# First layer's window-attention maxima: mask added and maximum taken per head by one VectorE instruction

## The chip, the cores and the metric

The kernel runs on one core of one Trainium2 chip. The metric is the device time of one execution in microseconds. A core has a matrix engine (TensorE, PE in the rows, with its weight loads as PEld), VectorE (DVE), ScalarE (ACT), GpSimd (POOL) and SyncE (SP), which starts most DMAs. TensorE writes only to PSUM, eight banks of 512 fp32 numbers per partition.

## What is computed

Two transformer layers over eight sequences ("batches") of 512 tokens by 256. The change lies in the first one, in its sliding-window attention (16 heads of 16, window 64):

```
scores = einsum('bqhd,bkhd->bhqk', q, k) / sqrt(D)
allowed = (t[None,:] <= t[:,None]) & (t[None,:] >= t[:,None] - WINDOW)
attn = softmax(where(allowed, scores, -inf)); win = attn @ v
lin  = linear_attention_causal(taylor(q @ Wqf), taylor(k @ Wkf), v)
x    = x + ga * (concat([lin, win]) @ Wout)        # then a gated feed-forward part
```

The second layer has causal softmax attention with rotary positions and a large feed-forward part (256 to 1024, 1024 to 1024 twice, and back).

## The kernel before, in words

**Quads.** Heads are handled four at a time; a batch has four such quads, so the first layer has 32. In `qT` and `kT` the four heads of a quad lie on four groups of 32 partitions, so that four products with 32 rows each share TensorE. One spare row of each head carries minus the row's maximum, so that the scores come out of TensorE with the maximum taken off and ScalarE needs only an `Exp`.

**Steps of a quad n.** `tq`, `tk` turn queries and keys; `fold` makes `mT` for the linear part; `wm.n.0` and `wm.n.1` make scores for the maxima, in two pieces (query tiles 0 to 2: widths 128, 192, 192 for each head; query tile 3: width 192); `again` turns the queries once more, now with the maxima in the spare row, and so waits for both `wm`; `lin.n.0/1/2` and `win.n.0/1` are the scores proper; `lv`, `wv` the products with the values; `lh`, `wh` the turn back. Per batch there are also `hT`, `qk`, `v` (norm and projections), `turn`, `out` (output projection), `xT`, `r`, `kk`, `last` (feed-forward), and `wt` steps that turn the second layer's weights.

**The wide room.** PSUM banks 0 to 3 form one room, "wide". `wm.n.0`, `wm.n.1`, `lin.n.0/1/2` and `win.n.0/1` all use it, seven fills per quad, one after another: a fill may begin only when the reader of the last one is done. ScalarE reads `lin` and `win` (lines 817 to 828), VectorE reads `wm` (lines 667 to 671). Banks 4 and 5 collect value products, banks 6 and 7 (`m0`, `m1`) take all other steps in turn.

**Mask and maximum before.** In `window_maxima` TensorE first multiplies the identity with the mask tile `bandr` (0 or -1e30), four products of 512 columns in `wm.n.0` and four of 192 in `wm.n.1` (line 976), and adds the score products to that (line 979). VectorE then takes the maxima with three wide reductions per quad (lines 667, 669, 671), writing minus the maximum.

**What sets the order.** Each engine runs its instructions in program order. One list of steps (the "plan") gives the order for all of them. It is unrolled from the tables `BODY0` and `BODY1`, one pass per batch, where `+1` or `+2` behind a step says that it runs that many passes later; the lists `START` and `TURN` replace the unrolled order at the beginning and where the layers meet. Until the second layer's feed-forward part can start, only its attention steps (`1:max`, `1:att`, in the same wide room) are there to run.

Of the kernel before, what the change touches and what calls it, by code (L numbers as in the profile page):

```python
# [140 lines left out]
tq.0 tk.0 win.3.1+1 turn.0+1 fold.0 wm.0.0 lv.3.1+1 lv.3.2+1 turn.2+1 wt.0+2 wm.0.1 wv.3.0+1 wv.3.1+1 lin.0.0 lh.3+1 v.0 again.0 lin.0.1 wh.3+1 v.1  # L141
win.0.0 turn.1+1 tq.1 lv.0.0 tk.1 lin.0.2 turn.3+1 fold.1 wm.1.0 out.0+1 wm.1.1 stats-1 out.1+1 mod again.1 lin.1.0 wv.0.0 lv.0.1 win.0.1 wt.1+2
lv.0.2 win.1.0 tq.2 lh.0 lv.1.0 lin.1.1 tk.2 fold.2 wv.0.1 wm.2.0 wt.2+2 rows.0-35 lv.1.1 wt.3+2 xT.0+1 rows.1+1 wm.2.1 flag+8 xg wh.0 xT.1+1 lin.1.2
wv.1.0 win.1.1 again.2 tq.3 lin.2.0 lv.1.2 r.0+1 lin.2.1 tk.3 fold.3 wv.1.1 lin.2.2 norm-1 lh.1 lv.2.0 wm.3.0 r.1+1 kk.0+1 wt.4+2 win.2.0 wh.1 kk.1+1
hT.0-1 wm.3.1 hT.1-1 wt.5+2 lv.2.1 rms-1 win.2.1 again.3 qk.0-1 qk.1-1 wt.6+2 lin.3.0 wv.2.0 wv.2.1 lv.2.2 lin.3.1 wh.2 qk.2-1 last.0+1 win.3.0 lh.2
last.1+1 qk.3-1 lin.3.2 lv.3.0
# [3 lines left out]
def first_layer(nc, ctx, room_ctx, kept, plan, fills, x_in_dram, norm_w, Wq, Wk, Wv, Wqf, Wkf, Wout, W_r, W_k, W_v, mu_r, mu_k, c, wmod, x_mid, next_weights, rope):  # L150
# [344 lines left out]
    def vector(dve):  # L495
# [66 lines left out]
        def run(step):  # L562
# [16 lines left out]
            elif name == "masks":  # L579
                dve.wait_ge(s_masks, 1)  # L580
                nc.vector.tensor_copy(kept.causalr[:], plain_causal)
                nc.vector.tensor_copy(bandr[:], plain_band).then_inc(s_round, 1)
# [577 lines left out]
h1.0.3.1+3 values.1.1+2 values.1.2+2 max.3.1+2 h2.0.0.0+3 h2.0.0.1+3 h2.0.1.0+3 att.2.0+2 h2.0.1.1+3 h2.0.2.0+3 max.3.2+2 h2.0.2.1+3 h2.0.3.0+3  # L1160
h2.0.3.1+3 att.2.1+2 heads.1+2 split.1+3 last.0.0+3 again.3+2 values.2.0+2 att.2.2+2 stats+1 values.2.1+2 att.3.0+2 last.0.1+3 values.2.2+2 att.3.1+2
heads.2+2 up.1.0+3 up.1.1+3 values.3.0+2 att.3.2+2 values.3.1+2 norm+1 up.1.2+3 up.1.3+3 values.3.2+2 hT+1 up.1.4+3 heads.3+2 up.1.5+3 proj.0+1
proj.1+1 up.1.6+3 tq.0+1 tk.0+1 proj.2+1 tq.1+1 tk.1+1 up.1.7+3 proj.3+1 tq.2+1 tk.2+1 h1.1.0.0+3 tq.3+1 tk.3+1 h1.1.0.1+3 h1.1.1.0+3 turn.0+2
max.0.0+1 h1.1.1.1+3 h1.1.2.0+3 max.0.1+1 h1.1.2.1+3 turn.1+2 h1.1.3.0+3 max.0.2+1 h1.1.3.1+3 out.0+2 again.0+1 max.1.0+1 h2.1.0.0+3 h2.1.0.1+3
out.1+2 att.0.0+1 h2.1.1.0+3 h2.1.1.1+3 max.1.1+1 h2.1.2.0+3 h2.1.2.1+3 h2.1.3.0+3 h2.1.3.1+3 xT+2 split.0+2 last.1.0+3 att.0.1+1 last.1.1+3
values.0.0+1 max.1.2+1 up.0.0+2 ga+1 up.0.1+2 att.0.2+1 up.0.2+2 again.1+1 max.2.0+1 up.0.3+2 up.0.4+2 values.0.1+1 values.0.2+1 att.1.0+1 up.0.5+2
up.0.6+2 att.1.1+1 heads.0+1 up.0.7+2 values.1.0+1 att.1.2+1 h1.0.0.0+2 max.2.1+1 h1.0.0.1+2 h1.0.1.0+2 h1.0.1.1+2 max.2.2+1 h1.0.2.0+2 h1.0.2.1+2
# [4 lines left out]
0:stats.0 0:norm.0 0:mod0.0 0:hT.0.0 0:masks.0 0:hT.0.1 0:rows.0.0 0:rms.0 0:qk.0.0 0:qk.0.1 0:qk.0.2 0:qk.0.3 0:wturn.0.0 0:tq.0 0:tk.0 0:fold.0  # L1172
0:wm.0.0 0:v.0.0 0:wm.0.1 0:wturn.0.1 0:wturn.0.2 0:lin.0.0 0:again.0 0:v.0.1 0:lin.0.1 0:lv.0.0 0:tq.1 0:tk.1 0:win.0.0 0:fold.1 0:xg.0 0:lv.0.1
0:wm.1.0 0:wt.0.0 0:wt.0.1 0:wv.0.0 0:wm.1.1 0:win.0.1 0:lin.0.2 0:again.1 0:tq.2 0:stats.1 0:lin.1.0 0:tk.2 0:wv.0.1 0:fold.2 0:lin.1.1 0:lv.0.2
0:lin.1.2 0:norm.1 0:wm.2.0 0:wh.0 0:lh.0 0:lv.1.0 0:wm.2.1 0:mod.0 0:win.1.0 0:hT.1.0 0:lv.1.1 0:lv.1.2 0:lin.2.0 0:win.1.1 0:again.2 0:wt.1.0
0:lin.2.1 0:wv.1.0 0:wv.1.1 0:lh.1 0:win.2.0 0:wh.1 0:tq.3 0:lv.2.0 0:win.2.1 0:tk.3 0:turn.0.0 0:lin.2.2 0:hT.1.1 0:fold.3 0:wm.3.0 0:wv.2.0 0:lv.2.1
0:wv.2.1 0:wm.3.1 0:lv.2.2 0:wh.2 0:rms.1 0:again.3 0:lin.3.0 0:qk.1.0 0:qk.1.1 0:win.3.0 0:qk.1.2 0:qk.1.3 0:lin.3.1 0:tq.4 0:lh.2 0:wv.3.0 0:lin.3.2
0:tk.4 0:fold.4 0:wm.4.0 0:v.1.0 0:lv.3.0 0:wm.4.1 0:lv.3.1 0:win.3.1 0:again.4 0:tq.5 0:lin.4.0 0:wv.3.1 0:lv.3.2 0:tk.5 0:lin.4.1 0:v.1.1 0:turn.0.2
0:lin.4.2 0:fold.5 0:lh.3 0:wm.5.0 0:wh.3 0:lv.4.0 0:lv.4.1 0:wm.5.1 0:turn.0.1 0:wt.1.1 0:lin.5.0 0:turn.0.3 0:again.5 0:tq.6 0:win.4.0 0:tk.6
0:lv.4.2 0:stats.2 0:fold.6 0:wm.6.0 0:out.0.0 0:wm.6.1 0:out.0.1 0:lin.5.1 0:lh.4 0:lv.5.0 0:xg.1 0:again.6 0:win.4.1 0:wv.4.0 0:win.5.0 0:lv.5.1  # L1180
0:tq.7 0:tk.7 0:lin.5.2 0:fold.7 0:win.5.1 0:xT.0.0 0:wv.4.1 0:norm.2 0:wm.7.0 0:wh.4 0:hT.2.0 0:wv.5.0 0:wv.5.1 0:wm.7.1 0:hT.2.1 0:rms.2 0:wh.5
0:win.6.0 0:again.7 0:qk.2.0 0:lv.5.2 0:win.6.1 0:qk.2.1 0:xT.0.1 0:lin.6.0 0:qk.2.2 0:qk.2.3 0:lin.6.1 0:lh.5 0:lv.6.0 0:wv.6.0 0:lin.6.2 0:wv.6.1
0:lv.6.1 0:lin.7.0 0:tq.8 0:v.2.0 0:win.7.0 0:tk.8 0:r.0.0 0:lv.6.2 0:lin.7.1 0:fold.8 0:v.2.1 0:win.7.1 0:r.0.1 0:wm.8.0 0:wh.6 0:lh.6 0:lv.7.0
0:wv.7.0 0:wm.8.1 0:kk.0.0 0:lin.7.2 0:kk.0.1 0:lin.8.0 0:lv.7.1 0:again.8 0:tq.9 0:lin.8.1 0:tk.9 0:fold.9 0:lv.7.2 0:wv.7.1 0:lin.8.2 0:last.0.0
0:win.8.0 0:lh.7 0:last.0.1 0:wh.7 0:wm.9.0 0:turn.1.0 0:lv.8.0 0:turn.1.2 0:turn.1.1 0:wm.9.1 0:lv.8.1 0:turn.1.3 0:again.9 0:win.8.1 0:lv.8.2
0:stats.3 0:tq.10 0:tk.10 0:lin.9.0 0:out.1.0 0:fold.10 0:wm.10.0 0:lh.8 0:out.1.1 0:lin.9.1 0:lv.9.0 0:wv.8.0 0:win.9.0 0:wv.8.1 0:lv.9.1 0:rows.0.1
0:xT.1.0 0:wm.10.1 0:wh.8 0:xT.1.1 0:lin.9.2 0:wv.9.0 0:win.9.1 0:again.10 0:tq.11 0:xg.2
# [4 lines left out]
0:win.26.1 0:norm.7 0:lv.26.1 0:wv.26.0 0:wm.27.0 0:hT.7.0 0:kk.5.0 0:hT.7.1 0:wm.27.1 0:kk.5.1 0:rms.7 0:lin.27.0 0:again.27 0:qk.7.0 0:wv.26.1
0:lv.26.2 0:win.27.0 0:qk.7.1 0:qk.7.2 0:wt.17.0 0:lin.27.1 0:lh.26 0:qk.7.3 0:win.27.1 0:lv.27.0 0:tq.28 0:tk.28 0:lin.27.2 0:fold.28 0:wh.26
0:wm.28.0 0:wv.27.0 0:v.7.0 0:lin.28.0 0:wt.17.1 0:v.7.1 0:wm.28.1 0:lv.27.1 0:wv.27.1 0:again.28 0:lin.28.1 0:tq.29 0:last.5.0 0:lin.28.2 0:lv.27.2
0:tk.29 0:wt.18.0 0:win.28.0 0:lh.27 0:fold.29 0:lv.28.0 0:wm.29.0 0:last.5.1 0:lv.28.1 0:wm.29.1 0:turn.6.0 0:turn.6.2 0:win.28.1 0:wt.18.1
# [856 lines left out]
```

## Time and profile before

| what | us |
|---|---|
| median of 3 runs | 2113.1 (2112.88 to 2118.12) |
| profiled execution, its own time | 2113.57 |
| span of its trace | 2111.8 |
| TensorE busy | 1993.2 (94%) |
| VectorE busy | 1241.8 (59%) |
| ScalarE busy | 943.9 (45%) |
| GpSimd busy | 519.5 (25%) |
| first layer | about 0 to 820 |
| layers meet, attention of the second alone | about 820 to 1000 |

The busy share of an engine is an average over stages with different limits. The timeline views give start, duration, engine, line and shape of instructions merged by form, and in brackets how long the engine had been idle and what ended that. From the start of one group to the start of the next on an engine that never idles is what a group costs it; the duration itself is some hundredths longer, since instructions overlap at their ends. One fp32 product is two records on TensorE, one fp32r product one record.

### The profile page before, as it was taken

The page shows a single profiled execution, that of the slowest core. Times are in us where ns is not written, and L with a number is a line of the kernel's source. Part 1 is how long each engine was busy: PE and PEld are TensorE (multiplying, and loading weights), DVE is VectorE, ACT ScalarE, POOL GpSimd, SP SyncE. Part 2 cuts the span into 40 slices and gives each one's busy share as a digit, 9 for nine tenths or more (in the row PEclk, how much of TensorE's full clock was granted, in tenths as well). Part 3 has the DMA queues.
Part 4 walks back from the last instruction along what each step waited for, and adds up shares of the span by engine and source line. Part 5 has one row for each costly group of instructions (what it writes and reads, how often), then busy time and mean ns, then how long its engine had stood idle before and what let it go on. Part 6 is the DMA issues. An engine that isn't in the chain of part 4 may idle for free.

```text
span 2111.8 us, 41909 instructions
## 1 busy us (share of the span) xinstructions
PE 1993.2 (94%) x17257; PEld 1456.0 (69%) x17257; DVE 1241.8 (59%) x2211; ACT 943.9 (45%) x1306; POOL 519.5 (25%) x676
## 2 busy tenths in 40 slices
...
GB/s 183 27 5 24 24 20 54 71 43 59 68 80 47 39 63 145 11 6 110 1 7 23 2 5 23 6 6 19 6 6 19 6 23 2 6 14 6 1 13 7
DMA packets 58030, 67.69 MB, mean 32 GB/s; under 512 B 11928, under 2 KB 48752, under 8 KB 57200
## 3 DMA queue, kind: packets, MB, share of 16 engines
...
q8 instruction: 141, 2.31, 0.5%
q14 instruction: 49, 0.40, 0.1%
...
## 4 chain that ended last, share of the span: by engine, by line
PE 82%; DVE 8%; ACT 6%; issue 2%; POOL 0%; SPq 0%; DMA 0%; ACTq 0%; DVEq 0%; POOLq 0%
PE ps L1886 28%; PE ps L1833 4%; PE ps L1821 4%; PE ps L1790 4%; PE ps L990 4%; PE ps L1022 3%; PE ps L1923 3%; PE ps L1849 3%; PE ps L1052 3%; PE ps L937 3%; ACT a_probs L817 3%; PE ps L1074 2%; PE ps L979 2%; PE ps L976 2%; PE ps L1000 2%
## 5 line engine op out<-in xcount | busy, mean ns | idle before, releaser
L1744 ACT ACTIVATE b_acts_exact<-ps,c_s 128x256 f32<-128x256 f32 x256 | 107.5, 471 | 373.6 <-PE ps L1886 373.4
L1886 PE MATMUL ps<-b_acts,b_h1T 128*128 128x256 f32 x2048 | 265.6, 287 | 2.7 <-POOL b_acts L1515 1.9
L1886 PEld LDWEIGHTS ps<-b_acts,b_h1T 128*128 128x128 f32 x2048 | 250.2, 191 | 23.0 <-issue 16.6
L1886 PEld LDWEIGHTS ps<-b_acts,b_h2T 128*128 128x128 f32 x2048 | 248.5, 192 | 20.9 <-issue 17.5
L1886 PE MATMUL ps<-b_acts,b_h2T 128*128 128x256 f32 x2048 | 257.8, 285 | 1.4 <-DVE b_acts L1658 1.4
L439 POOL TENSOR_SCALAR_AFFINE_SELECT a_probs<-a_probs 128x512 f32<-128x512 f32 (+1 forms) x224 | 161.3, 736 | 386.4 <-ACT a_probs L817 225.6
L1507 POOL TENSOR_SCALAR_AFFINE_SELECT b_work<-b_work 128x512 f32<-128x512 f32 x128 | 80.7, 642 | 515.5 <-ACT b_work L1708 515.5
L1708 ACT ACTIVATE b_work<-ps 128x2048 f32<-128x2048 f32 (+1 forms) x96 | 153.2, 1596 | 95.9 <-PE ps L1833 95.1
L817 ACT ACTIVATE a_probs<-ps 128x2048 f32<-128x2048 f32 (+1 forms) x96 | 153.1, 1595 | 84.1 <-PE ps L990 72.9
L1579 DVE TENSOR_REDUCE c_nat<-ps 128x4 f32<-128x2048 f32 (+3 forms) x128 | 188.0, 1490 | 3.3
L1657 DVE CAST b_acts<-b_acts_exact 128x512 fp32r<-128x512 f32 x128 | 55.2, 431 | 218.1 <-ACT b_acts_exact L1744 217.8
L1515 POOL TENSOR_TENSOR b_acts<-c_nat,b_acts 128x256 fp32r<-128x256 f32 x128 | 94.8, 741 | 261.3 <-DVE b_acts L1650 261.3
L1022 PE MATMUL ps<-a_probs,c_va 128*17 128x192 f32 (+4 forms) x2048 | 131.8, 379 | 1.0 <-POOL a_probs L439 0.8
L1821 PE MATMUL ps<-c_kT,c_qT 32*128 32x512 f32 (+3 forms) x1024 | 102.1, 492 | 26.8 <-DVE c_nat L1579 18.7
L1576 DVE TENSOR_TENSOR ps<-ps,c_causalr 128x512 f32<-128x512 f32 x128 | 86.0, 695 | 68.7 <-PE ps L1821 68.4
L1833 PE MATMUL ps<-c_qT,c_kT 32*128 32x512 f32 (+3 forms) x1024 | 98.1, 475 | 19.9 <-DVE c_nat L1579 10.1
L990 PE MATMUL ps<-a_mT,c_kT 32*128 32x512 f32 (+3 forms) x1024 | 99.6, 482 | 10.2 <-DVE c_nat L671 3.8
L1886 PE MATMUL ps<-b_acts,b_w1T 128*128 128x256 f32 x512 | 92.6, 303 | 13.1 <-DVEq L1649 9.3
L1737 ACT ACTIVATE c_nat<-ps,c_s 128x256 f32<-128x256 f32 x128 | 59.6, 475 | 101.3 <-PE ps L1886 71.0
L1886 PEld LDWEIGHTS ps<-b_acts,b_w1T 128*128 128x128 f32 x512 | 69.5, 189 | 36.9 <-DVEq L1649 22.2
L1022 PEld LDWEIGHTS ps<-a_probs,c_va 128*17 128x17 f32 x2048 | 47.6, 97 | 64.1 <-issue 52.4
L1658 DVE TENSOR_TENSOR b_acts<-b_acts_exact,b_acts 128x512 fp32r<-128x512 f32 x128 | 88.7, 693 | 4.4
...
## 6 DMA issues: line engine op xcount, KB each, us to landing
...
```

Source lines behind the costliest of these rows:

```text
L439: return nc.gpsimd.affine_select(out=z, in_=z, compare_op=ALU.is_ge, fill=0.0, base=0, pattern=[[0, blocks_n], [1, cols]], channel_multipl ...
L817: nc.scalar.activation(pb, here[:, :, 0:w], ACT.Square, bias=1.0, scale=0.5).then_inc(att_ready, 1)
L990: ins = nc.tensor.matmul(here[:, i, o:o + S - kb * P], kT[rows_of(i), n % RING, kb * P:(kb + 1) * P], mT[rows_of(i), n % RING, kb * P:S], ...
L1022: ins = nc.tensor.matmul(here[R * i:R * i + HD + 1, kb * P:kb * P + q], va[:, b % 2, kb, 4 * g + i, :], pb[:, first + i * pitch:first + i ...
L1515: nc.gpsimd.tensor_tensor(act_a[:, i, 1], th[i % 2], act_a[:, i, 0].bitcast(F32), ALU.subtract).then_inc(a_ready, 1)
L1579: ins = nc.vector.tensor_reduce(nat[:, t, 0, 4 * g:4 * g + 4, HD:HD + 1], room["wide"][:, :, o:o + (t + 1) * P], AX.X, ALU.max, negate=True)
L1658: nc.vector.tensor_tensor(dst[:, :, 1], z, dst[:, :, 0].bitcast(F32), ALU.subtract).then_inc(h_split, 1)
L1708: ins = nc.scalar.activation(probs[nth % 2][:, 0:4 * w].rearrange("p (h q) -> p h q", q=w), here[:, :, 0:w], ACT.Exp, scale=float(HD) ** -0.5)
L1744: ins = nc.scalar.activation(dst[:, j], here[:, j * HALF:(j + 1) * HALF], ACT.Gelu, scale=s12[:, 2 + (name == "h2"), 2 * i + j:2 * i + j + 1])
L1821: ins = nc.tensor.matmul(here[:, i, o:o + (t + 1) * P], qT[rows_of(i), g, t * P:(t + 1) * P], kT[rows_of(i), g, 0:(t + 1) * P], start=True ...
L1833: ins = nc.tensor.matmul(here[:, i, o:o + S - kb * P], kT[rows_of(i), g, kb * P:(kb + 1) * P], qT[rows_of(i), g, kb * P:S], start=True, st ...
L1886: ins = nc.tensor.matmul(dst, view(w[:, m, k]), view(src[:, k, i]), start=(k == 0 and i == 0), stop=(k == nk - 1 and i == 1))
```

## The change

The mask products are gone. `band` is now an ordinary fp32 tile, and for each head and query tile one `tensor_tensor_reduce` on VectorE adds the mask to the scores in PSUM, multiplies by -1 and keeps the minimum, written straight to the spare row. The window-score products start their own sums (`start=True`). All order tables are replaced (`BODY0`, `BODY1`, `START`, `TURN`), and a third list `END` fixes the last two batches of the second layer. The tables are cut here; what they move is shown below.

```diff
-    bandr = sb("bandr", [P, 512], F32R)
+    band = sb("band", [P, 512])
...
-                if step[2] == 0:
-                    nc.vector.tensor_reduce(nat[:, 0, 0, 4 * g:4 * g + 4, HD:HD + 1], here[:, :, 0:P], AX.X, ALU.max, negate=True)
-                    to = nat[:, 1:3, 0, 4 * g:4 * g + 4, HD].rearrange("p t h -> p h t")
-                    nc.vector.tensor_reduce(to, here[:, :, P:512].rearrange("p h (t q) -> p h t q", q=192), AX.X, ALU.max, negate=True).then_inc(free, 1)
-                else:
-                    nc.vector.tensor_reduce(nat[:, 3, 0, 4 * g:4 * g + 4, HD:HD + 1], here[:, :, 0:192], AX.X, ALU.max, negate=True).then_inc(free, 1)
+                if b == 0:
+                    dve.wait_ge(s_round, 1)
+                for t, o, first, w in WIN_MAX[step[2]]:
+                    lo = 0 if t == 0 else P
+                    for i in range(4):
+                        part = here[:, i, o:o + w]
+                        ins = nc.vector.tensor_tensor_reduce(part, part, band[:, lo:lo + w], -1.0, -NEG, ALU.add, ALU.min, nat[:, t, 0, 4 * g + i, HD:HD + 1])
+                ins.then_inc(free, 1)
...
-            lo, w = ((0, 512), (P, 192))[j]
-            if n + j == 0:
-                pe.wait_ge(s_round, 1)
-            for i in range(4):
-                nc.tensor.matmul(here[:, i, 0:w], identr[:], bandr[:, lo:lo + w], start=True, stop=False, skip_group_check=True)
...
-                                           kT[rows_of(i), n % RING, first:first + width], start=False, stop=(t >= 2), skip_group_check=True)
+                                           kT[rows_of(i), n % RING, first:first + width], start=True, stop=True)
...
-ORDERS = (START, TURN,)
+ORDERS = (START, TURN, END,)
```

TensorE, before, around `wm.17.1`, the second piece of the maxima of batch 4's second quad (line 1052 is `out`, 957 `again`, 990 the next `lin`):

```order
L1052 MATMUL ps<-a_wout,a_oT 128x256 x8
L976 MATMUL ps<-a_bandr,c_identr 128x192 x4
L979 MATMUL ps<-c_kT,c_qT 128x192 x4
L1052 MATMUL ps<-a_wout,a_oT 128x256 x8
L957 MATMUL ps<-c_identr,c_nat 128x128 x4
L990 MATMUL ps<-a_mT,c_kT 128x512 x4
```

TensorE, changed kernel, the same step (line 977; line 988 is `lin.16.2`, 1038 `turn`, 1084 `wt`, 998 `win.16.1`):

```order
L1084 MATMUL ps<-c_identr,a_raw_next 128x128 x4
L977 MATMUL ps<-c_kT,c_qT 128x192 x4
L988 MATMUL ps<-a_mT,c_kT 128x256 x4
L1038 MATMUL ps<-c_identr,a_onat 128x128 x4
L1084 MATMUL ps<-c_identr,a_raw_next 128x128 x4
L998 MATMUL ps<-c_qT,c_kT 128x192 x4
```

Before, `out` and `again` lay between this piece and the next fill of the wide room; now that fill (`lin.16.2`) follows at once.

TensorE, changed kernel, around both pieces of the next quad (line 1050 is `out`, 1030 `lh`, 988 `lin.17.2`):

```order
L1030 MATMUL ps<-c_identr,a_sums 128x128 x4
L977 MATMUL ps<-c_kT,c_qT 128x128 x4
L977 MATMUL ps<-c_kT,c_qT 128x192 x8
L1050 MATMUL ps<-a_wout,a_oT 128x256 x8
L977 MATMUL ps<-c_kT,c_qT 128x192 x4
L1050 MATMUL ps<-a_wout,a_oT 128x256 x8
L988 MATMUL ps<-a_mT,c_kT 128x256 x4
```

The first `out` step now stands between the two pieces of quad 18, the second behind them; before, they stood there in quad 17.

VectorE, before, at that `out` step (557 and 558 gate and add, 525 and 528 are the statistics):

```order
L667 TENSOR_REDUCE c_nat<-ps 128x4
L669 TENSOR_REDUCE c_nat<-ps 128x4x2
L557 TENSOR_TENSOR ps<-ps,a_ga 128x512
L558 TENSOR_TENSOR a_x<-a_x,ps 128x512
L525 BN_STATS a_stats<-a_x 128x6 x2
L528 BN_AGGR a_meanvar<-a_stats 128x2 x2
L671 TENSOR_REDUCE c_nat<-ps 128x4
```

VectorE, changed kernel, the end of the twelve pairs of `wm.18.0`, the `out` step (558, 559, 526, 529), and the first of the four pairs of `wm.18.1`:

```order
L673 ISA ps,c_nat<-ps,a_band 128x192
L673 ISA c_nat 128x1
L558 TENSOR_TENSOR ps<-ps,a_ga 128x512
L559 TENSOR_TENSOR a_x<-a_x,ps 128x512
L526 BN_STATS a_stats<-a_x 128x6 x2
L529 BN_AGGR a_meanvar<-a_stats 128x2 x2
L673 ISA ps,c_nat<-ps,a_band 128x192
L673 ISA c_nat 128x1
```

Each `tensor_tensor_reduce` is a pair of instructions, the pass over the columns and a read of the accumulator, so three reductions per quad have become 32 instructions.

## Rows read from the trace of the kernel before

**Rows 1.** The page's first part: busy time (share of the span) and instructions.
```profile
PE 1993.2 (94%) x17257; PEld 1456.0 (69%) x17257; DVE 1241.8 (59%) x2211; ACT 943.9 (45%) x1306; POOL 519.5 (25%) x676
```

**Rows 2.** Windows: stretch, length, busy PE, PEld, DVE, ACT, POOL (instructions), granted clock.
```profile
300.00:400.00 100.00, 97.85 (x932) 61.59 (x928) 58.34 (x102) 54.94 (x71) 37.51 (x47) 1.00 0.17 51
...
50.00:110.00 60.00, 51.30 (x481) 32.52 (x477) 24.28 (x56) 32.70 (x42) 22.59 (x26) 0.80 0.09 28
...
820.00:1000.00 180.00, 134.55 (x856) 80.07 (x855) 114.02 (x190) 51.62 (x67) 20.43 (x28) 0.85 0.19 74
```

**Rows 3.** Groups of instructions by form: busy us, mean ns | idle before, releaser.
```profile
L976 PE MATMUL ps<-a_bandr,c_identr 128*128 128x512 f32 x128 | 40.5, 439 | 2.5 <-ACTq L819 1.2 <-ACTq L831 0.8
L667 DVE TENSOR_REDUCE c_nat<-ps 128x4 f32<-128x512 f32 x32 | 22.2, 693 | 70.8 <-PE ps L979 70.7
L669 DVE TENSOR_REDUCE c_nat<-ps 128x8 f32<-128x1536 f32 x32 | 56.0, 1749 | 0.0
L671 DVE TENSOR_REDUCE c_nat<-ps 128x4 f32<-128x768 f32 x32 | 30.6, 955 | 12.6 <-PE ps L979 12.4
L817 ACT ACTIVATE a_probs<-ps 128x2048 f32<-128x2048 f32 x64 | 120.2, 1878 | 60.8 <-PE ps L990 51.1 <-DVE a_wvT L598 8.1 <-ACT a_xT L853 0.2
L817 ACT ACTIVATE a_probs<-ps 128x1024 f32<-128x1024 f32 x32 | 32.9, 1028 | 23.4 <-PE ps L990 21.8 <-ACT c_nat L803 1.0 <-ACT a_xT L853 0.4
L824 ACT ACTIVATE a_probs<-ps 128x1536 f32<-128x1536 f32 x32 | 46.5, 1453 | 36.5 <-PE ps L1000 36.2 <-ACT a_staged L765 0.2
L826 ACT ACTIVATE a_probs<-ps 128x512 f32<-128x512 f32 x32 | 19.0, 592 | 0.0
L828 ACT ACTIVATE a_probs<-ps 128x768 f32<-128x768 f32 x32 | 26.0, 812 | 27.6 <-PE ps L1000 27.1 <-ACT c_nat L803 0.2 <-ACT a_staged L765 0.2
```

**Rows 4.** TensorE's timeline in three batches: start, duration, operation.
```profile
435.16 1.17 PE L976 MATMUL ps<-a_bandr,c_identr 128*128 128x512 f32 x3
...
440.13 0.69 PE L976 MATMUL ps<-a_bandr,c_identr 128*128 128x192 f32 x4
440.75 0.61 PE L979 MATMUL ps<-c_kT,c_qT 32*128 32x192 f32 x8
...
454.14 0.66 PE L1040 MATMUL ps<-c_identr,a_onat 128*128 128x128 f32 x4
454.63 1.02 PE L965 MATMUL ps<-c_qT,a_fold 128*128 128x512 f32 x2
455.40 1.20 PE L976 MATMUL ps<-a_bandr,c_identr 128*128 128x512 f32 x4
456.52 1.16 PE L979 MATMUL ps<-c_kT,c_qT 32*128 32x128 f32 x24
457.61 3.72 PE L1052 MATMUL ps<-a_wout,a_oT 128*128 128x256 f32 x16
...
534.09 1.18 PE L976 MATMUL ps<-a_bandr,c_identr 128*128 128x512 f32 x3
```

**Rows 5.** VectorE's timeline at the `out` step of batch 3.
```profile
458.36 1.75 DVE L669 TENSOR_REDUCE c_nat<-ps 128x8 f32<-128x1536 f32 x1
...
464.08 0.96 DVE L671 TENSOR_REDUCE c_nat<-ps 128x4 f32<-128x768 f32 x1
464.95 1.39 DVE L525 BATCH_NORM_STATS2 a_stats<-a_x 128x6 f32<-128x256 f32 x4
466.38 0.38 DVE L528 BATCH_NORM_AGGREGATE a_meanvar<-a_stats 128x2 f32<-128x6 f32 x4
```

**Rows 6.** ScalarE's timeline: the only accumulator reads in the trace.
```profile
499.65 0.42 ACT L784 ACTIVATE a_sq<-a_h 128x256 f32<-128x256 f32 x1 [1.80 <-DVE a_h L644]
499.97 0.19 ACT L784 ACTIVATION_READ_ACCUMULATOR a_sq<-a_h 128x1 f32 x1
500.19 0.42 ACT L784 ACTIVATE a_sq<-a_h 128x256 f32<-128x256 f32 x1
```

**Rows 7.** Waits of TensorE from 820 to 1000 us: in total, times, longest.
```profile
PE ps L1821 <- DVE c_nat L1579: 18.7, 6, 4.0
```

More of the change, by code:

```diff
@@ L140 @@
 BODY0 = """
[L141 to L146, printed above, removed]
+again.1+2 tq.2+2 lin.1.0+2 wv.0.0+2 lv.0.2+2 tk.2+2 lin.1.1+2 turn.3+3 fold.2+2 lh.0+2 wm.2.0+2 out.0+3 wm.2.1+2 out.1+3 lin.1.2+2 xg+2 lv.1.0+2
+wv.0.1+2 lin.2.0+2 lv.1.1+2 again.2+2 tq.3+2 win.1.0+2 wh.0+2 lv.1.2+2 tk.3+2 win.1.1+2 lh.1+2 wt.2+3 lin.2.1+2 lv.2.0+2 fold.3+2 lin.2.2+2 xT.0+3
+wt.3+3 norm+1 wm.3.0+2 wv.1.0+2 hT.0+1 hT.1+1 rms+1 lv.2.1+2 wv.1.1+2 lv.2.2+2 rows.1+2 wm.3.1+2 wt.4+3 rows.0-17 xT.1+3 win.2.0+2 again.3+2 qk.0+1
+lin.3.0+2 qk.1+1 r.0+3 qk.2+1 lin.3.1+2 flag+27 lh.2+2 qk.3+1 r.1+3 tq.0+1 win.2.1+2 tk.0+1 fold.0+1 wm.0.0+1 wh.1+2 v.0+1 lv.3.0+2 wv.2.0+2 wv.2.1+2
+wm.0.1+1 kk.0+3 lin.3.2+2 mod+1 again.0+1 kk.1+3 lin.0.0+1 tq.1+1 tk.1+1 lv.3.1+2 lv.3.2+2 win.3.0+2 lh.3+2 last.0+3 lin.0.1+1 last.1+3 v.1+1
+win.3.1+2 wh.2+2 fold.1+1 wm.1.0+1 turn.0+2 wt.5+3 wv.3.0+2 lv.0.0+1 wv.3.1+2 turn.2+2 wt.6+3 win.0.0+1 wh.3+2 lv.0.1+1 wt.0+2 wm.1.1+1 lin.0.2+1
+turn.1+2 wt.1+2 win.0.1+1 stats
 """
@@ L581, in run @@
                 nc.vector.tensor_copy(kept.causalr[:], plain_causal)
[L582 removed]
+                nc.vector.tensor_copy(band[:], plain_band).then_inc(s_round, 1)
                 nc.vector.memset(lows[:], 0.0).then_inc(lows_zero, 1)
@@ L1159 @@
 BODY1 = """
[L1160 to L1167, printed above, removed]
@@ L1169 @@
 """
 START = """
[L1172 to L1187, printed above, removed]
+0:stats.0 0:norm.0 0:wturn.0.0 0:mod0.0 0:masks.0 0:hT.0.0 0:hT.0.1 0:rows.0.0 0:rms.0 0:qk.0.0 0:qk.0.1 0:qk.0.2 0:qk.0.3 0:xg.0 0:wturn.0.1 0:tq.0
```

91 lines of the change are left out of this document (64 added, 27 removed).

## Prediction

> **What bounds the kernel now.** I read the busy shares first, then the same by stretch, then the timelines of TensorE and VectorE in a steady stretch, then the waits. TensorE is busy 94% of the span, VectorE 59% [rows 1]. In the steady part of the first layer TensorE is busy 97.85 of 100 us at full clock while VectorE is busy 58 [rows 2]: TensorE sets the pace there. The same place in the plan comes at 435.16 and at 534.09 [rows 4], so a batch takes 98.9 us and a quad 24.7. From 820 to 1000 us TensorE is busy only 134.6 of 180 us [rows 2]; its largest wait there is for the second layer's own maxima on VectorE, 18.7 us [rows 7], which the change leaves alone.
>
> Behind TensorE the next resource is the wide room, which no view names. Per quad its fills cost TensorE 1.12 + 1.09 us for `wm.0` (455.40 to 456.52 to 457.61) and 0.62 + 0.53 for `wm.1` (0.62 from 440.13 to 440.75; the 0.61 long product less its overlap of 0.08) [rows 4]; the five fills of `lin` and `win`, of the same form and widths as these products, add 4.4 (by the products here: 1.07 for a full room twice, 0.65, 1.08, 0.54; an estimate within 0.2). The readers take 0.61 + 1.75 (the two reductions overlap by 0.08) and 0.96 on VectorE, and 2 x 1.88, 1.03, 1.45 + 0.59 less 0.1, and 0.81 on ScalarE [rows 3]: 10.9 together. Seven hand-overs at 0.15 to 0.22 add 1.5. That is 20.1 of 24.7 us, with 4.6 us to spare.
>
> **What is removed.** The mask products cost TensorE 1.12 + 0.62 = 1.74 us per quad [rows 4], on the engine that sets the pace; nothing hides them. All 32 quads have them (128 records of the 512 wide form [rows 3]): 32 x 1.74 = 55.7 us. If nothing else moved, this would be the gain, 2057 us.
>
> **What is added.** Three reductions (3.3 us per quad) become 12 pairs over 192 columns and 4 over 128. The trace has no such pair. Its column pass is bounded from rows: a column costs 1.03 ns, from 693 ns for 512 and 1749 for 1536 [rows 3]. Four statistics over 256 columns take 1.39 us in a row [rows 5], so one starts 0.32 after the other, 0.06 beyond its columns. By that 192 columns cost 0.26 and 128 cost 0.19 if passes overlap; alone and without any overlap 0.36 and 0.30 (693 less 320 or 384 columns). For the accumulator read the nearest low row is the short aggregates, four in 0.38 [rows 5], 0.08 each; the high one ScalarE's own read, 0.19 long [rows 6]. There the read starts 0.32 after the pass over 256 columns, before that pass's recorded end of 0.42, so the two do overlap, and 0.22 passes to the next (with a wait between). So a pair costs 0.34 and 0.27 at the cheap end (5.2 us per quad), 0.55 and 0.49 at the dear end (8.6). I take 0.36 and 0.29, near the cheap end because both rows of back-to-back work show overlap: 12 x 0.36 + 4 x 0.29 = 5.5 us per quad, 4.0 for the first piece and 1.4 for the second. It can't be below today's 3.3, since no fewer columns are read.
>
> VectorE itself can bear it: 2.2 us more per 24 us raises 58% to about 67%. The Trainium skill ("Vector Engine (DVE) Microarchitecture Reference", measured stream behaviour) puts a fixed 75 ns on every instruction after overlap, custom programs included; by it the pair would be 0.35 and 0.29, and the sum the same.
>
> **What the longer reads cost.** They hold the wide room. Fills fall by 1.74 and readers grow by 2.2 per quad, so its use is 20.1 - 1.7 + 2.2 = 20.6 us out of TensorE's 24.7 - 1.7 = 23.0: 2.4 us to spare in place of 4.6. Whether TensorE stalls then hangs on what the plan puts between a fill and the next one. I added this up over the plan: at each fill, the reader's time plus 0.22 less the TensorE work placed before the next fill; what is positive is a stall.
>
> Before, in a batch like the fifth, these sum to 0.7 us on 98.5 of work, 99.2 in all against 98.9 in the trace, so the adding is fair. After, work is 91.5. The four first pieces have 5.1, 4.9, 3.56 and 4.4 us of work behind them and the reader needs 4.0 + 0.22: only quad 18, with one `out` (3.56 counted, 3.4 here from 457.61 to 460.98) between its pieces, stalls, by 0.7. The four second pieces need 1.44 + 0.22 and have 1.7, none, 3.56 and 1.0: a stall of 1.66 where `lin.16.2` follows `wm.17.1` at once, and one of 0.64. The other fills, whose readers on ScalarE are as before, now have less work behind them and stall 1.7. Sum 4.7: a batch takes 96.2 in place of 99.2, a gain of 3.0.
>
> The same adding over the whole first layer, with the new lists at its two ends, gives stalls of 61.4 against 18.8, and 43.2 against 41.0 where the layers meet (the attention fills wait for each other there in both plans). So 55.7 - 42.6 - 2.2 = 10.9 us gained. At the cheap pair it is 15.4, at 0.39 and 0.32 it is 1.9, and it passes zero near 0.40. At the dear end stalls reach 145 us and the kernel is 73 us slower, 2186.
>
> **Queues.** VectorE works in order. At `out` today the third reduction starts at 464.08 [rows 5], behind the gate and statistics of `out`. In the new plan the 24 instructions of `wm.18.0` stand ahead of that `out`, and its gate and statistics (some 2.4 us) ahead of the four pairs of `wm.18.1`; the `out` behind covers most of this. `tk` copies, turn-backs and the second norm wait behind bursts of 4.0 us where they waited behind 2.4. I put 2 us on all of it (0 to 15). On ScalarE and GpSimd nothing is added. The wait for the mask's copy moves from TensorE to VectorE, which made the copy itself: nothing. The setup copy to plain fp32 costs as before. `mod` moves ahead to the second quad's place; its inputs are loaded by then if they land as now. `END` reorders work of a stage in which TensorE is the bound: 0 to 2 us, taken as 0.
>
> **Clock.** From 50 to 110 us TensorE was granted 0.80 [rows 2], a mix of its two levels, 2.4 and 1.2 GHz, after the waits of the first quads. That is at most 12 us. The new start may win a few of them or lose as many; 5 either way in the range.
>
> **Sum.** 2113.6 (the profiled execution, 0.5 above the median) - 10.9 + 2 gives 2104.7, and from the median 2104. Forecast: **2104 us**, some 0.4% faster.
>
> **Rivals.** (1) *The pair is dear.* If the accumulator read waits until the pass has left the pipe and the next pass waits for the read, the cost goes to the dear end. It decides from 0.40 us per pair; at 0.45, halfway, the sum is about +30, 2143. For it: the read needs the last element's result, and TensorE then waits at nearly every `wm`. Against it: rows 5 and 6. The Trainium skill ("VectorE: DVE Perf Modes", the DRAIN section) says that the next op doesn't start until the pipe is empty, and its errata section warns that many small tiles each pay the fixed latency and advises 512 elements or more; that speaks against this change. The trace disagrees with the first in part, with four statistics in 1.39 us, and has no accumulator read on VectorE. Chance 0.20, and 0.07 more that VectorE's queue alone costs 15 to 25 us: slower either way.
> (2) *The room hides better than my adding.* It counts each stall in full; a late reader can be made up where the next gap is wide. Then half of the 42.6 stays away: 2083. Chance 0.20. That it all stays away, 2057, has 0.03.
> (3) *An even trade.* Pairs of 0.37 to 0.41, or 5 to 10 us in queues: 2107 to 2119. Chance 0.13. That the work isn't removed is excluded: the order holds no mask product.
> The forecast itself (2097 to 2110) has 0.37, of which some 0.11 lies within the bound below.
>
> **Numbers.** A measurement can tell about 0.3%, 6.3 us. Faster by more: 0.26 + 0.20 + 0.03 = 0.49. Within: 0.11 + 0.13 = 0.24. Slower: 0.27. The range takes in rival 2 and the dear pair up to its middle: 2076 to 2145; about 0.1 lies below and 0.1 above.
>
> **What would show it.** Right: line 673's passes start about 0.36 us apart, TensorE's busy time falls by some 50 us, and its waits for line 673 and for the ScalarE readers grow to about 60 us before 790. Wrong: pairs above 0.40; waits of TensorE on other VectorE work (`tk`, turn-backs); a change in the stretch after 1000 us; a granted clock at the start far from 0.80. The batch period should be near 96 us.

## The result, and the profile after

The changed kernel takes **2098.3 us** (median of 4 runs, 2096.3 to 2099.2) where the kernel before, run beside it, takes 2115.6 (median of 4). The ratio is 0.992, with a 95% interval of 0.990 to 0.993: some 0.8% faster. The four runs of the kernel before lie at two levels, 2113 and 2118 us, so the medians are 17.3 us apart and the two profiled executions (2113.6 and 2098.5), which the splits below use, 15.1. The forecast was 2104. It lies 6 us off, inside the range, but the parts behind it don't agree nearly as well as the sum.

The page's first part, of the changed kernel (span 2096.6 us, profiled execution 2098.5), answers to [rows 1]:

```profile
PE 1961.9 (94%) x17001; PEld 1428.7 (68%) x17001; DVE 1304.1 (62%) x3139; ACT 957.5 (46%) x1316; POOL 522.1 (25%) x676
```

TensorE is busy 31.3 us less, not 50; part of the difference is work that ran at a lower clock (below). The windows of the changed kernel, the first three for the stretches of [rows 2], the others 690 and 800 us long (columns: stretch, length, busy PE, PEld, DVE, ACT, POOL, then the granted clock of TensorE):

```profile
300.00:400.00 100.00, 94.84 (x909) 59.01 (x912) 67.73 (x217) 56.12 (x74) 38.48 (x46) 0.97 0.18 57
50.00:110.00 60.00, 47.70 (x476) 27.92 (x475) 29.11 (x116) 33.30 (x41) 19.07 (x26) 0.85 0.10 23
820.00:1000.00 180.00, 138.72 (x901) 82.54 (x900) 114.82 (x177) 54.33 (x70) 21.35 (x29) 0.86 0.17 68
110.00:800.00 690.00, 648.07 (x6279) 395.77 (x6278) 450.17 (x1492) 381.92 (x485) 266.46 (x326) 0.98 0.15 47
1000.00:1800.00 800.00, 796.57 (x6742) 641.01 (x6742) 522.86 (x948) 369.26 (x522) 149.43 (x202) 1.00 0.04 11
```

The same two long stretches of the kernel before:

```profile
110.00:800.00 690.00, 671.81 (x6451) 419.75 (x6451) 375.15 (x636) 375.27 (x479) 262.83 (x325) 1.00 0.15 46
1000.00:1800.00 800.00, 788.88 (x6675) 635.31 (x6676) 526.07 (x931) 351.82 (x507) 144.34 (x197) 1.00 0.04 10
```

Three things stand there. In the first layer TensorE's idle time grew from 18.2 to 41.9 of 690 us, and its clock fell. From 1000 to 1800 us, where I expected no change at all, idle time fell from 11.1 to 3.4 us. So I split each run at one instruction, the last record of the last turn back of the first layer's sums (`L1032`, then `L1030`): it starts at 820.2 us before and at 814.5 after. The first layer gave 5.7 us, and what lies behind it took 1291.6 us before and 1282.1 after: 9.5 us, the larger part.

VectorE's timeline at `wm.16.0` of the changed kernel (start, duration, operation, what it waited for); passes over 128 columns with their accumulator reads, then two over 192:

```profile
442.86 0.14 DVE L673 DVE_READ_ACCUMULATOR2_ANT c_nat<- 128x1 f32 x1
442.86 0.33 DVE L673 CUSTOM_DVE_ANT_0 ps<-ps,a_band 128x128 f32<-128x128 f32 x1
443.11 0.14 DVE L673 DVE_READ_ACCUMULATOR2_ANT c_nat<- 128x1 f32 x1
443.11 0.33 DVE L673 CUSTOM_DVE_ANT_0 ps<-ps,a_band 128x128 f32<-128x128 f32 x1
...
444.24 0.40 DVE L673 CUSTOM_DVE_ANT_0 ps<-ps,a_band 128x192 f32<-128x192 f32 x1
444.55 0.14 DVE L673 DVE_READ_ACCUMULATOR2_ANT c_nat<- 128x1 f32 x1
444.55 0.40 DVE L673 CUSTOM_DVE_ANT_0 ps<-ps,a_band 128x192 f32<-128x192 f32 x1
```

Read the starts: one pass follows the other after 0.25 us (128 columns) and 0.315 (192), and each accumulator read stands at the same start as the next pass. A quad's pairs cost 12 x 0.315 + 4 x 0.25 = 4.8 us, cheaper than the cheap end of the prediction (5.2), against 3.3 for the three reductions. Still TensorE waits for them:

```profile
PE ps L988 <- DVE c_nat L673: 11.7, 11, 1.5
PE ps L1030 <- DVE a_onat L551: 7.6, 4, 2.0
PE ps L1030 <- DVE c_kT L663: 6.1, 2, 3.2
PE ps L998 <- DVE c_nat L673: 5.7, 7, 1.5
```

These are TensorE's largest waits from 100 to 800 us (in total, times, longest). The second and third are the "other VectorE work" that the prediction listed as a sign against it. TensorE's waits for line 673 and for the readers on ScalarE come to 36 us before 790 (18 in the kernel before), where the prediction said about 60.

### The profile page after: what moved, and what is told of

It is laid out like the page before. It is cut to its first block, busy times and chain, and to the rows that moved or that the text cites. A ratio compares the mean times of both kernels' runs of the same rounds, so it can differ in the third digit from the quotient of the medians.

```text
span 2096.6 us, 42338 instructions
## 1 busy us (share of the span) xinstructions
PE 1961.9 (94%) x17001; PEld 1428.7 (68%) x17001; DVE 1304.1 (62%) x3139; ACT 957.5 (46%) x1316; POOL 522.1 (25%) x676
## 4 chain that ended last, share of the span: by engine, by line
PE 82%; DVE 7%; ACT 5%; issue 4%; POOL 1%; SPq 0%; DMA 0%; ACTq 0%; DVEq 0%; POOLq 0%
PE ps L1899 29%; PE ps L1834 4%; PE ps L1846 4%; PE ps L1020 4%; PE ps L988 4%; PE ps L1803 4%; PE ps L1862 4%; PE ps L1936 3%; PE ps L940 3%; PE ps L1072 3%; PE ps L977 2%; PE ps L998 2%; ACT a_probs L820 2%; DVE ps L673 2%; PE ps L960 2%
## 5 line engine op out<-in xcount | busy, mean ns | idle before, releaser
L1899 PE MATMUL ps<-b_acts,b_h2T 128*128 128x256 f32 x2048 | 262.9, 286 | 1.4 <-DVE b_acts L1671 1.4
L1899 PE MATMUL ps<-b_acts,b_h1T 128*128 128x256 f32 x2048 | 260.9, 286 | 1.8 <-POOL b_acts L1528 1.1
L1899 PEld LDWEIGHTS ps<-b_acts,b_h1T 128*128 128x128 f32 x2048 | 249.4, 191 | 18.2 <-issue 14.8
L1899 PEld LDWEIGHTS ps<-b_acts,b_h2T 128*128 128x128 f32 x2048 | 249.9, 191 | 16.0 <-issue 11.1
L673 DVE CUSTOM_DVE_ANT_0 ps<-ps,a_band 128x192 f32<-128x192 f32 (+1 forms) x512 | 156.3, 378 | 57.6 <-PE ps L977 57.1
L1834 PE MATMUL ps<-c_kT,c_qT 32*128 32x512 f32 (+3 forms) x1024 | 100.8, 487 | 28.3 <-DVE c_nat L1592 18.2
L988 PE MATMUL ps<-a_mT,c_kT 32*128 32x512 f32 (+3 forms) x1024 | 100.7, 486 | 21.5 <-DVE c_nat L673 13.2
L988 PEld LDWEIGHTS ps<-a_mT,c_kT 32*128 32x128 f32 x1024 | 45.0, 191 | 70.0 <-DVE c_nat L673 21.5
```

Of the source, the lines that this page charges most:

```text
L673: ins = nc.vector.tensor_tensor_reduce(part, part, band[:, lo:lo + w], -1.0, -NEG, ALU.add, ALU.min, nat[:, t, 0, 4 * g + i, HD:HD + 1])
L988: ins = nc.tensor.matmul(here[:, i, o:o + S - kb * P], kT[rows_of(i), n % RING, kb * P:(kb + 1) * P], mT[rows_of(i), n % RING, kb * P:S], ...
L1834: ins = nc.tensor.matmul(here[:, i, o:o + (t + 1) * P], qT[rows_of(i), g, t * P:(t + 1) * P], kT[rows_of(i), g, 0:(t + 1) * P], start=True ...
L1899: ins = nc.tensor.matmul(dst, view(w[:, m, k]), view(src[:, k, i]), start=(k == 0 and i == 0), stop=(k == nk - 1 and i == 1))
```

## Experiments

All medians are set against the kernel before, run on the same chip (2113.7 to 2114.9 us). "End of layer 1" is the start of the last turn back in the profiled run, "rest" the span behind it. These two come from one execution each, and executions of one kernel lie up to 8 us apart (e5: 2062.6 to 2070.7), so a difference of a few microseconds between two rows isn't firm by itself.

| run | time, us | ratio (95%) | end of layer 1 | rest |
|---|---|---|---|---|
| before | 2115.6 | 1 | 820.2 | 1291.6 |
| changed | 2098.3 | 0.992 (0.990-0.993) | 814.5 | 1282.1 |
| e1 order alone | 2128.4 | 1.006 (1.004-1.008) | 845.4 | 1280.8 |
| e2 operation alone | 2118.6 | 1.002 (1.001-1.003) | 826.5 | 1289.2 |
| e3 new first, old second | 2109.7 | 0.997 (0.996-0.998) | 816.8 | 1292.2 |
| e4 old first, new second | 2106.7 | 0.996 (0.995-0.998) | 820.0 | 1282.4 |
| e5 no mask, old order | 2066.8 | 0.977 (0.975-0.979) | 777.3 | 1291.6 |
| e6 no mask, new order | 2078.7 | 0.983 (0.982-0.985) | 794.1 | 1284.0 |
| e7 dear passes | 2138.4 | 1.012 (1.010-1.013) | 855.9 | 1284.2 |
| e8 gate behind `wh` | 2122.3 | 1.004 (1.003-1.006) | 833.1 | 1282.3 |
| e9 no mask, old first, new second | 2058.8 | 0.974 (0.972-0.975) | 777.1 | 1282.6 |
| e10 gate one fill later | 2099.6 | 0.993 (0.992-0.995) | 816.1 | 1282.5 |
| e11 the same, no mask | 2081.4 | 0.985 (0.983-0.986) | 799.4 | 1283.2 |
| e12 e4 without END | 2104.5 | 0.995 (0.994-0.997) | 822.3 | 1281.7 |

### Which half of the change, and which half of the program

**e1** keeps the mask products and takes all new tables; **e2** takes the new operation and keeps all old tables.

```diff
 e1, in the kernel before:
-ORDERS = (START, TURN,)
+ORDERS = (ALL,)
 e2, in the changed kernel:
-ORDERS = (START, TURN, END,)
+ORDERS = (ALL,)
```

`ALL` is one list of every step, in e1 in the changed kernel's order, in e2 in that of before.

> The kernel before (mask products on TensorE, three wide reductions) with all of the new order (both bodies, START, TURN, END). Theory A (the order of the second layer carries some 9 us of the 15 gained, the new order of the first layer is made for fills without mask products): my adding of the wide room over this plan gives 85 us of stalls where the kernel before has 59, so the first layer is up to 26 us longer, less 9 in the second layer: 2120 to 2133. Theory B (the order carries nothing, the operation all of it): 2114 within 3.

> The changed operation (16 passes per quad on VectorE, no mask products) with all of the old order. Theory A: the second layer's 9 us are not gained; by the adding at the measured 0.315 and 0.25 us per pass the first layer has 85 us of stalls against 59 before, so it gains 55.7 - 26 = 30 us at most, and the clock takes some of that back: 2085 to 2100. Theory B (the new first-layer order is needed to cover the longer reads): 2105 or more.

e1 came out inside the span of theory A (2128). e2 refutes theory A's size for the first layer (2085 to 2100) and bears out theory B there: at 2118.6 the operation alone gains nothing, so the longer reads need the new first-layer order. Removing the products and adding the longer reads cancel in the old order. Neither half of the change is faster by itself; both together are. But e1 and e2 take both layers' orders at once; the next two runs part them.

**e3** and **e4** cut the order at the first step of the second layer.

```diff
 ALL of e3
+steps of the changed order up to 1:stats.0, then the rest as before
 ALL of e4
+steps of the order before up to 1:stats.0, then the rest as changed
```

> The changed kernel with its order up to the first step of the second layer, and from there on the steps in the old order. Theory A (the second layer's order carries 9 us): 2107 to 2110, the last product of the first layer at 814 as in the changed kernel, and the gain after it gone. Rival C (the later gain only follows from where the first layer leaves the queues): 2098 to 2101.

> The kernel before, mask products and old order up to the first step of the second layer, and from there on the steps in the new order. Theory A: 2104 to 2107, that is 9 us faster than before with nothing changed in the first layer. Rival C: 2113 to 2116.

Both fit theory A, and the gain is found where it should be: the rest is 1292.2 us in e3 and 1282.4 in e4, by the order there and not by the first layer. TensorE's waits from 1000 to 1800 us in the kernel before:

```profile
PE ps L1833 <- DVE c_nat L1579: 4.6, 5, 0.9
PE ps L1886 <- DVEq L1649: 4.5, 10, 0.7
PE ps L1821 <- ACTq L1711: 2.0, 1, 2.0
PE ps L1833 <- ACTq L1711: 1.2, 6, 0.2
```

and in e4, with the same instructions in the new order (`L1970` is the fill that `L1833` was):

```profile
PE ps L1937 <- issue: 2.5, 6, 0.4
PE ps L1970 <- ACTq L1848: 0.3, 1, 0.3
```

12.3 us of waits became 2.8. **e12** takes `END` out of e4 again:

```diff
 the new order behind 1:stats.0 in e4
-ORDERS = (START, TURN, END,)
+ORDERS = (START, TURN,)
```

> As the run with the old first layer and the new order behind it (2106.7), but with the list END left out, so that the last steps fall where the repeated order puts them. Theory A as it now stands (the second layer's gain is in its repeated order, where 12.3 us of waits between 1000 and 1800 became 3): 2105 to 2109, END is worth within 2. Rival J (END carries the gain, or is needed to keep it): 2112 or more.

2104.5 against 2106.7: `END` is worth nothing. The 9 us are in the repeated order `BODY1` (with the part of `TURN` that leads into it, which no run parts from it). The other way round there is no time: with the new `END` and all else as before, the engines come to wait for each other for good (a deadlock), so that kernel doesn't end.

### What the longer reads cost

**e5** and **e6** leave the mask out of the maxima and keep the three wide reductions, so TensorE is relieved and VectorE reads as briefly as before. A maximum over more keys still only shifts the exponents.

```diff
-            for i in range(4):
-                nc.tensor.matmul(here[:, i, 0:w], identr[:], bandr[:, lo:lo + w], start=True, stop=False, skip_group_check=True)
...
-                                           kT[rows_of(i), n % RING, first:first + width], start=False, stop=(t >= 2), skip_group_check=True)
+                                           kT[rows_of(i), n % RING, first:first + width], start=True, stop=True)
```

> The kernel before in its old order with the mask products left out: the maxima are taken by the same three wide reductions over scores that are not masked (the part left out is the mask in the maxima alone; the scores of the softmax are masked as before). So TensorE is relieved of 1.74 us per quad and the reads are no longer. Theory A (each us taken off TensorE comes back but for the stalls that the adding finds, 59 as before, and for what the clock takes): 55.7 less 10 to 20 of clock and queues, 2072 to 2082. Rival D (the wide room takes most of it even with short reads): above 2090.

> The same without mask products and with the three wide reductions, in all of the new order. Against the changed kernel only the longer reads are gone. Theory A: the adding gives 9 us fewer stalls than for the changed kernel at 0.315 us per pass: 2086 to 2092. Rival E (the clock and VectorE's queue, not the reads, hold the changed kernel): 2096 to 2099.

Both were faster than theory A said. In e5 the first layer ends 42.9 us earlier, although its first `fold` comes 3.9 us later (40.4 for 36.5), and a steady batch takes 92.6 us (one `fold` to the same four quads later, 417.97 to 510.58 below) where it took 98.9 [rows 4]:

```profile
417.97 1.02 PE L965 MATMUL ps<-c_qT,a_fold 128*128 128x512 f32 x2
...
510.58 1.02 PE L965 MATMUL ps<-c_qT,a_fold 128*128 128x512 f32 x2
```

That is 6.3 of the 7.0 us (4 x 1.74) that the products' rows add up to. The rest of the pairs' story is the difference between runs that share an order:

- Old order: e2 minus e5 is the longer reads alone, 4.8 in place of 3.3 us per quad, 48 us in all. The first layer gets 49.2 us longer: the reads are paid in full.
- New order: the changed kernel minus e6 is the same step, and costs 20.4 us.

The steady part says the same. The mean of three batches, from the 13th `fold` to the 25th, is 92.4 us in e5 and 99.8 in e2 (7.4 more for 6 us of reading), 95.5 in e6 and 98.0 in the changed kernel (2.5 more), against 98.9 before.

**e7** lengthens the reads once more, by one reduction of a constant tile ahead of each tile's four passes:

```diff
                 for t, o, first, w in WIN_MAX[step[2]]:
+                    k = 4 * b + t
+                    nc.vector.tensor_reduce(dump[:, k:k + 1], band[:, 0:256], AX.X, ALU.max)
+                for t, o, first, w in WIN_MAX[step[2]]:
```

> The changed kernel with one reduction over 256 columns more, of a constant tile, ahead of each tile's four passes: four of about 0.32 us per quad, so a pass costs 0.40 in the mean, where the prediction put the point without gain. Theory A: the adding gives 24 us more of stalls: 2118 to 2126. Rival F (TensorE makes up late reads and the pair's price hardly matters): 2100 to 2106.

2138.4, dearer than both theories. Three of the reductions took 1.06 us in a row, so four per quad are some 1.4 us, 45 us in all, and the first layer got 41.4 us longer. The new order covers 6 tenths of the first lengthening and a tenth of the next. The prices hold more than waits: by the granted clock (next section) between 110 and 800 us, up to 12 of the 49.2 us and 10.5 of the 20.4 are lower clock, and none of the 41.4.

Why the old order covers nothing shows in TensorE's timeline of e2 at `wm.16`: the first piece is filled at 440.7, and the second piece waits for its readers:

```profile
439.56 1.16 PE L977 MATMUL ps<-c_kT,c_qT 32*128 32x128 f32 x24
440.65 1.49 PE L1020 MATMUL ps<-a_probs,c_va 128*17 128x384 f32 x24
442.07 0.66 PE L1038 MATMUL ps<-c_identr,a_onat 128*128 128x128 f32 x4
442.56 0.60 PE L1084 MATMUL ps<-c_identr,a_raw_next 128*128 128x128 f32 x4
444.47 0.61 PE L977 MATMUL ps<-c_kT,c_qT 32*128 32x192 f32 x8 [1.31 <-DVE c_nat L673]
```

There are 2.5 us of work behind the fill, and 3.6 of reading. Of the 28 first pieces between 110 and 790 us the next wide fill came within 0.35 us of the last pass in all 28 in e2, and in 13 of 28 before and after the change. That is what the new first-layer order buys: it puts more work behind `wm.0`. It is no good order for its own sake. With short reads it costs 16.8 us (e6 against e5), with the mask products 25.2 (e1 against before), and only with the long reads it gains, 12.0 us (changed against e2).

### The clock, and a step beside GpSimd

TensorE's timeline of the changed kernel in one batch, then in the next, at the same place:

```profile
384.57 0.66 PE L1030 MATMUL ps<-c_identr,a_sums 128*128 128x128 f32 x4 [2.01 <-DVE a_onat L551]
385.17 1.11 PE L1084 MATMUL ps<-c_identr,a_raw_next 128*128 128x128 f32 x4
386.21 2.09 PE L988 MATMUL ps<-a_mT,c_kT 32*128 32x384 f32 x16
...
482.06 0.66 PE L1030 MATMUL ps<-c_identr,a_sums 128*128 128x128 f32 x4 [1.86 <-DVE a_onat L551]
482.66 0.66 PE L1084 MATMUL ps<-c_identr,a_raw_next 128*128 128x128 f32 x4
483.25 1.15 PE L988 MATMUL ps<-a_mT,c_kT 32*128 32x384 f32 x16
```

Behind the first wait the eight products of `L988` (16 records) take 2.09 us, behind the second 1.15. In the first case the granted clock was at its lower level, 1.2 GHz, for a few microseconds, in the second it was not. The windows show it for the first, and for the stretch that holds the second:

```profile
380.00:390.00 10.00, 7.62 (x58) 3.87 (x56) 9.74 (x14) 5.47 (x6) 9.26 (x9) 0.83 0.08 28
...
410.00:510.00 100.00, 94.50 (x916) 58.42 (x909) 67.60 (x215) 57.54 (x73) 39.00 (x48) 1.00 0.19 57
```

It is 0.83 from 350 to 360 as well, behind a wait of 1.49 us for line 673. Added up in windows of 10 us over 110 to 800, each with its length times what its granted clock lacks of 1, what is missing is 3.2 us before, 17.3 after, 13.6 in e2, 17.0 in e7, 6.8 in e6 and 1.7 in e5. By and large the runs in which TensorE idles more lose more clock, but not in proportion: it is idle 41.9 of the 690 us in the changed kernel, 39.1 in e6 and 64.4 in e7. Which wait is followed by a fall isn't settled: of the two above one was, the other wasn't.

The wait of 2.01 us had its cause in VectorE's queue. VectorE's timeline there:

```profile
377.61 6.29 DVE L695 TENSOR_SCALAR a_xn<-a_x,a_meanvar,a_rstd 128x256 f32<-128x256 f32 x4 [1.13 <-POOL a_rstd L436]
```

and GpSimd's:

```profile
378.31 2.36 POOL L467 TENSOR_TENSOR a_h<-a_h,a_ga 128x1024 f32<-128x1024 f32 x1
380.75 2.36 POOL L468 TENSOR_TENSOR a_x<-a_x,a_h 128x1024 f32<-128x1024 f32 x1
```

The new order puts `xg` (these two passes) one fill behind `out.1`. VectorE's four short passes then end only when GpSimd's two are over: the first and the last take 0.71 and 0.72 us, the two between them 2.58 and 2.51, each about as long as one of GpSimd's. Over the whole run they take 1.33 us each, where they took 0.74 before. The Trainium skill ("Trainium Architecture — The Big Picture", what this means for kernel authors) says that the port pair shared by VectorE and GpSimd is taken as an exclusive lock and not as a split; the two long passes agree. It comes with the new order and not with the longer reads: in e6, with short reads, the same passes take 1.34 us each, and the waits of TensorE are as long:

```profile
PE ps L1030 <- DVE a_onat L550: 7.6, 4, 2.0
PE ps L1030 <- DVE c_kT L662: 6.5, 2, 3.3
```

In the old order (before, e2, e5) a wait of this kind comes once, with 4.1 or 4.2 us for `a_onat`, early on, and those for `kT` stay under 1 us. **e8** moves `xg` behind the next `wh` in all batches but the first, **e10** only behind the next `lin` fill (six batches), and **e11** is e10 with the operation of e6. The edits are written in the terms of the table; the runs hold them in the unrolled list.

```diff
 e8
-out.1+3 lin.1.2+2 xg+2 lv.1.0+2 wv.0.1+2 lin.2.0+2 lv.1.1+2 again.2+2 tq.3+2 win.1.0+2 wh.0+2
+out.1+3 lin.1.2+2 lv.1.0+2 wv.0.1+2 lin.2.0+2 lv.1.1+2 again.2+2 tq.3+2 win.1.0+2 wh.0+2 xg+2
 e10, e11
-out.1+3 lin.1.2+2 xg+2 lv.1.0+2 wv.0.1+2 lin.2.0+2
+out.1+3 lin.1.2+2 lv.1.0+2 wv.0.1+2 lin.2.0+2 xg+2
```

> The changed kernel with one step moved: the residual with the gate (xg, two GpSimd passes of 2.36 us over fp32 in SBUF) stands a few steps later, behind the next wh, and no longer right behind out.1, whose four normalising passes on VectorE took 6.29 us beside it instead of some 2.6. Theory G (the two engines shut each other out, TensorE then waits 2.0 us for VectorE once per batch, and half of the half-speed stretches of 3.41 us follow from these waits): the passes of line 695 go from 1.59 to about 0.65 us in the mean, the half-speed stretches of the steady part from eight to four or fewer, the time to 2086 to 2092. Rival H (another wait comes in its place): 2096 to 2099.

> The changed kernel with the residual and gate step (xg) moved behind the next lin fill in six of the eight batches, that is behind one select on GpSimd, and not behind the next wh, where the second norm then waited for it. Theory G (the 2.0 us wait of TensorE per batch and the half-speed stretches behind it come from VectorE's passes at line 695 beside xg): these passes take 2.0 us for four in place of 6.3, the time 2086 to 2092. Rival I (xg ends some 4 us later and the first pass of the norm, which had 4.5 us to spare behind it, waits): 2098 to 2104.

> As the run before with the new order, but with the three wide reductions over unmasked scores (the mask left out of the maxima alone). Theory G: 2078.7 less 2 us in each of the six batches: 2067 or less. Rival I: 2079 or more.

In all three the four waits for `a_onat` behind this step went, and the time did not. e8 is 24 us slower than the changed kernel: the norm overwrites `a_h`, which `xg` reads, so VectorE now waits for GpSimd, and TensorE for the normed tile. VectorE's largest wait from 200 to 800 us in e8:

```profile
DVE a_h L641 <- POOL a_x L468: 41.9, 6, 15.9
```

and TensorE's from 100 to 800:

```profile
PE ps L929 <- DVE a_h L645: 21.7, 5, 5.8
```

In e10, on VectorE's timeline, the four passes take 2.00 us, but the norm's own, now beside GpSimd's selects, take longer (3.40 and 3.05 for four, where the changed kernel has 2.56 and 2.43):

```profile
377.28 2.00 DVE L695 TENSOR_SCALAR a_xn<-a_x,a_meanvar,a_rstd 128x256 f32<-128x256 f32 x4 [1.13 <-POOL a_rstd L436]
...
385.98 3.40 DVE L641 SCALAR_TENSOR_TENSOR a_h<-a_x,a_meanvar,a_hg 128x256 f32<-128x256 f32 x4
389.41 3.05 DVE L645 SCALAR_TENSOR_TENSOR a_h<-a_h,a_rstd,a_hg 128x256 f32<-128x256 f32 x4
```

TensorE's waits for the normed tile (6.1 us in ten waits) took the place of those for `a_onat`. A steady batch takes 96.7 or 96.8 us at full clock with the collision and without it (changed kernel, e10), and 95.5 in both kernels with short reads (e6, e11). Rival I is right in its time, theory G falls: that the collision happens is shown, that it costs the kernel anything is not.

### A version that beats both

**e9** puts together what had gained by itself: e5's maxima over unmasked scores, the old first-layer order, the new second-layer order (the edits of e5 and e4).

> No mask products, the three wide reductions over scores that are not masked (the mask is left out of the maxima alone), the old order up to the second layer's first step and the new order behind it. If the parts add up: 2066.8 of the run with the old order throughout, less 8 to 9 for the second layer's new order: 2058. If the second layer's new order needs the changed first layer ahead of it: 2066.

2058.8, as the parts add up to: 2.6% faster than before and 1.9% than the changed kernel. The mask isn't needed in the maxima as long as no masked score lies so far above the others that the exponents underflow. It is a different trade in numbers: a row whose largest score is a masked one loses headroom.

## Why the prediction was right, and where it was wrong

- **What is removed: 1.74 us per quad, 55.7 in all.** Too large as a gain. Without longer reads a steady batch gains 6.3 of 7.0 us, the whole first layer 42.9 (e5). From the first `fold` to the 13th, where the first three batches wait for each other, it gave 14.0 of 21.
- **The pair: 5.5 us per quad.** Mis-sized, in the dear direction: 4.8. The read adds no step of its own; with 1.03 ns for a column [rows 3] a pair has some 0.12 us beyond its columns. Rival 1 falls: the next pass starts 0.25 us after one that is recorded with 0.33. The Trainium skill ("Vector Engine (DVE) Microarchitecture Reference", measured stream behaviour) puts some 75 ns on an instruction behind another. For the pass and the read together that would be 0.15 us, an estimate by that page; the timeline shows 0.12.
- **What the longer reads cost.** The mechanism is right, a second use of the wide room behind TensorE, and it was shown by e2, e5 and e7. The size is not. For the first layer alone the adding gave 17.6 us of gain at 5.2 us per quad and 13.1 at 5.5 (its 15.4 and 10.9, with the 2.2 lost where the layers meet added back); carried on to the measured 4.8 that is some 23 (an estimate), and for e2 it gave 30. Measured are 5.7 and a loss of 6.3. It leaves out the clock and the queues of the next two points, and it took the products' removal at its full 1.74 us. Place by place it holds well: `lin.16.2` behind `wm.17.1` waits 1.49 us, predicted 1.66, and 1.48 with the measured pair; in quad 18, behind `out`, TensorE waits 0.1 in place of 0.7, and 0.16 with the measured pair. The batch from 415.8 to 512.5, which has full clock, takes 96.7 us, predicted 96.2. That is closer than it should be: with the measured pair the same adding gives 95.3, and a wait of 1.86 us for `a_onat` stands in this batch that it doesn't know. The neighbours, at a granted clock of 0.97 each, take 98.8 and 98.6, so a steady batch gains 0.9 us in the mean of the three and not 3.0.
- **Queues: 2 us (0 to 15).** Too small, and with another cause. TensorE waits 13.7 us for the `a_onat` division and the `kT` copy (the two middle rows of the waits). The prediction had turn-backs and copies wait behind the longer bursts of maxima; e6 has the same waits, 14.1 us, with the short ones, and the old order has some 5 us of them, with long reads (e2) or short (before, e5). So they belong to the new order.
- **Clock: 5 us at the start, nothing later.** The start was right (0.85 in place of 0.80). That the new small waits would be followed by the lower clock in the steady part was missing: 14 us more than before.
- **"`END` ... taken as 0", and no change after 1000 us.** `END` is 0 indeed (e12). But the diff also changes `BODY1`, and I gave it no term. It brings 9 us, more than half of what the changed kernel gains. The waits that it takes away, 12.3 us, stood in the trace of before; I had not listed them.

So the forecast was 6 us too slow, as a sum of misses that partly cancel: behind the first layer 9.5 us were gained where the sum had 2.2 lost, and the first layer gave 5.7 us in place of 11.1 (13.1 less 2 for the queues). That the sum came out so close is luck. None of the rivals describes it. The forecast's own case has the right mechanism in the first layer and the wrong account of where the microseconds lie.
